# Row numbers, softmax factors and a scale read from a PSUM bank, and messages made four steps at once, in a graph and expert kernel

## The chip, the cores and the metric

The kernel runs on one core of one Trainium2 chip. The time is that of one execution on the device, in microseconds. Before the change it was 4558.61 us, the median of 3 runs (4550.4 to 4563.28).

## The reference

12,500 nodes with 256 features, 200,000 edges sorted by destination. Three blocks on the normalized rows, with residuals:

```python
xn = layernorm(x)
# 1 graph attention, 4 heads of 64
h = (xn @ W_src).reshape(n, 4, 64); a_src = (h * att_src).sum(-1); a_dst = ((xn @ W_dst).reshape(n, 4, 64) * att_dst).sum(-1)
e = leaky_relu(a_src[src] + a_dst[dst], 0.2)
p = exp(e - segment_max(e, dst)[dst])
out = segment_sum(p / segment_sum(p, dst)[dst] * h[src], dst) + bias     # then layernorm, prelu
# 2 linear attention with elu+1 features (8 heads of 32), merge, layernorm, a two-layer relu block on [xn, msg], layernorm(g2, b2)
# 3 eight experts of three layers with batch norm and relu, mixed by a softmax over the mean features
x = x + gat(xn) + mix(xn);  x = x + experts(layernorm(x))
```

## The kernel before, in words

There are three stages. A projection (up to about 340 us) computes the products of all nodes in chunks of 512 and writes the table `h_tab` (4 heads of 64 values and one source logit each, 260 words a node). Then comes the edge stage, and last the expert stage. The change is in the edge stage alone.

**Edge stage.** The edges are cut into 1664 steps of up to 128 edges, each of one destination tile of 128 nodes. 32 steps (`GS`) are a turn, and 4 steps (`GU`) a block `b`, so a turn has 8 blocks (`GQ`) and there are 52 turns. In turn g the engines aggregate the edges of turn g ("here") and prepare the softmax of turn g+1 ("ahead", q in the code); gathers and row numbers run up to two turns ahead. The second block, mix, advances in the same turns: one chunk of 512 nodes takes two turns, sixteen slots i = 0..15, so that even turns carry slots 0 to 7 and odd turns 8 to 15. These pairs of turns are what the rows below show. Slots 12 to 15 hold the four `hidden` products (L1487), 2 and 9 the output products (L1500), 7 and 8 `merge` (L1465).

**Order.** Nothing plans it: each engine has one function `turn` in which its work is written out by hand, block by block, and semaphores order the engines (`Stage.wait`, with counts per turn). Queues are first in, first out.

- POOL gathers the 128 rows of a step with one indirect DMA (L857) into `G[s]`, one of two buffers; it waits only for the aggregation of the same block two turns earlier (`g_mm`).
- DVE makes the one-hot matrices of a block (`onehot`, L391: the row of numbers 0 to 127 compared with each edge's relative destination), the chain of maxima, the logits (`dst_sums`, `exponents`, L935 to L949), the terms that shrink the running sum (`shrink`, L953 to L960; `shrunk`, L968), the weighted rows (`message`, L976: two steps at once, each gathered row times its softmax factor, which ACT has put in the row's 65th column) and the running sum (`add`, L991, each one on the one before it). It also serves mix: `o_scale` (L1043) times g2, `o_finish` (L1049) adds to the base, `quotients` (L1011), `deviations` (the norm's twelve small operations).
- ACT reads the source logits out of the gathered rows (`sources`, L1194, waits for all 32 gathers of the next turn), takes the exponent (L1208), turns a one-hot block to f32 (L1188) and empties PSUM for mix.
- PE transposes one-hots (L1338), looks up logits (L1349), aggregates (L1362: one-hot by weighted rows, step k into PSUM bank k mod 4, after the add that last read that bank) and computes mix's products. Banks 0 to 3 are used by the aggregation, 5 by mix.

Within a block DVE's order is: `message` of the next block's first half, add 0, `message` of its second half, add 1, the piece of work ahead, the mix slot, add 2, `onehot`, add 3, the rest of the mix slot. In the last block of a turn `dst_sums` and `exponents` stand first, then adds 0 and 1, `shrink` and both first messages of the next turn.

Of the kernel before, what the change touches and what calls it, by code (L numbers as in the profile page):

```python
# [5 lines left out]
P = 128  # L6
D = 256
HEADS = 4
KD = D // P
CH = 4  # L10
# [58 lines left out]
def build(nc, a, out, N, E):  # L69
# [13 lines left out]
    with es:  # L83
# [215 lines left out]
        T4 = ps[4][:, 0:D].bitcast(bf16)  # L299
        LB = 5  # L300
# [10 lines left out]
        o_norm, o_g, o_base = stage("o_norm"), stage("o_g"), stage("o_base")  # L311
# [15 lines left out]
        msg_set, g_mm, acc_add = stage("msg_set", 2 * GQ), stage("g_mm", GS), stage("acc_add", GS)  # L327
# [57 lines left out]
        def onehot(dve, q, sq, b):  # L385
# [6 lines left out]
                                    iota_row[:, :].unsqueeze(1).broadcast_to([P, GU, P]), d, ALU.is_equal  # L392
# [88 lines left out]
        def project_vector(dve):  # L481
# [133 lines left out]
            onehot(dve, 0, 0, 0)  # L615
            onehot(dve, 0, 0, 1)
# [190 lines left out]
        with nc.Block() as block:  # L807
# [55 lines left out]
            def _(dve):  # L863
# [13 lines left out]
                dve.wait_ge(ed_set, 1)  # L877

# [92 lines left out]
                def message(g, s, b, i):  # L971
# [69 lines left out]
                def o_scale(c):  # L1041
                    o_norm.wait(dve, c)
                    nc.vector.tensor_tensor(TM, TM, row(R_G2).unsqueeze(1).broadcast_to([P, CH, D]),  # L1043
                                            ALU.mult).then_inc(o_g.sem, 1)

                def o_finish(c):
                    o_g.wait(dve, c)
                    bx_in.wait(dve, c)
                    nc.vector.tensor_tensor(BX, BX, TM, ALU.add).then_inc(o_base.sem, 1)  # L1049

                def mix_between(n, i):
# [12 lines left out]
                    if prev and i == 14:  # L1064
                        o_scale(n - 1)
                    if prev and i == 15:
                        o_finish(n - 1)

                def mix_after(n, i):
# [4 lines left out]
                    if cur and i in (4, 5):  # L1074
                        quotients(n, i - 4)

                def turn(g, s, n, q, sq, nq, r):
# [5 lines left out]
                    for b in range(GQ):  # L1083
# [5 lines left out]
                        if here:  # L1089
                            if b < GQ - 1:  # L1090
                                message(g, s, b + 1, 0)
                            add(g, s, b, 0)
                            if b < GQ - 1:
                                message(g, s, b + 1, 1)
                            add(g, s, b, 1)
                        if ahead:
# [12 lines left out]
                            if b == GQ - 1:  # L1109
                                shrink(q, sq)  # L1110
                                message(q, sq, 0, 0)
# [995 lines left out]
```

## Time and profile before

| | us |
|---|---|
| median of the runs | 4558.61 |
| the profiled execution | 4551.85 |
| its span | 4549.9 |
| PE / DVE / ACT / POOL busy | 4134.0 / 3823.0 / 2277.0 / 1888.1 |
| mean granted clock of TensorE | 0.953 |

Busy times are sums over the span. A group of instructions has a line of the kernel, its count, its busy time and mean length, and the idle time of its engine just before it with what ended that. On a timeline, rows of the same kind that follow one another are merged; "x2" then means two, and the length runs from the first start to the last end.

### The profile page before, as it was taken

To read this page: it belongs to the slowest core of one execution; us is meant where nothing else is said; L and a number is where in the kernel's file an instruction comes from. 1 tells how busy PE (TensorE), PEld (TensorE's weight loads), DVE (VectorE), ACT (ScalarE), POOL (GpSimd) and SP (SyncE) were. 2 spreads that over 40 slices of the span, in tenths; PEclk is the share of its full clock that TensorE was granted. 3 is DMA by queue.
4 is the path that set the end of the run, shared out by engine and by line. 5 is a ranking of instruction groups with operands and counts; after the bars stand their busy time and mean duration, and the time that the engine had idled before them with its cause. 6 is when DMAs were issued, how large, how long until landed. Compare 5 with 4: busy or idle time off the path is not lost. (4 is left out here: it accounts for less than half of the span.)

```text
span 4549.9 us, 85744 instructions
## 1 busy us (share of the span) xinstructions
PE 4134.0 (91%) x23003; PEld 3316.4 (73%) x23004; DVE 3823.0 (84%) x9879; ACT 2277.0 (50%) x4346; POOL 1888.1 (41%) x1702
## 2 busy tenths in 40 slices
PE   8984898889988988998898884999999999999999
PEld 7873666666666666666666653888888888888888
DVE  8875889888988899898989886787887878878786
ACT  5552344344334334443434333666666666666666
POOL 2117777777777777777777730000000000000000
PEclk9996999999999999999999987999999999999999
DMA  5545777777777777777777753000000000000000
GB/s 193 170 142 149 206 205 227 213 209 208 226 211 208 210 223 208 208 221 218 210 206 220 211 164 93 23 21 28 14 28 20 22 28 14 28 24 19 28 14 19
DMA packets 440077, 601.76 MB, mean 132 GB/s; under 512 B 41560, under 2 KB 366704, under 8 KB 439920
## 3 DMA queue, kind: packets, MB, share of 16 engines
q1 hardware_dynamic: 360048, 378.47, 25.8%
q0 software_dynamic: 79872, 221.62, 19.7%
q8 instruction: 47, 0.77, 0.1%
q14 instruction: 110, 0.90, 0.1%
HBM read 312.68 MB, written 287.25 MB: 132 GB/s over the span
## 5 line engine op out<-in xcount | busy, mean ns | idle before, releaser
L857 POOL DMA_INDIRECT acc<-h_tab,strips x1664 | 1824.0, 1096 | 538.4 <-issue 518.0
L1362 PE MATMUL ps<-acc 128*128 128x260 f32 x3328 | 1011.1, 432 | 24.1 <-DVE acc L991 16.1
L991 DVE SCALAR_TENSOR_TENSOR acc<-acc,strips,ps 128x260 f32<-128x260 f32 x1664 | 792.4, 476 | 208.2 <-PE ps L1362 176.8
L1362 PEld LDWEIGHTS ps<-acc 128*128 128x128 f32 x3328 | 621.0, 207 | 112.7 <-DVE acc L991 22.4
L976 DVE TENSOR_TENSOR acc<-acc 128x512 f32<-128x512 f32 x832 | 562.6, 681 | 0.0
L1896 ACT ACTIVATE exp<-ps,bn 128x512 f32<-128x512 f32 (+1 forms) x400 | 310.2, 775 | 452.7 <-PE ps L1963 449.0
L1961 PE MATMUL ps<-w_hi,b_hi 128*128 128x256 f32 x1568 | 444.8, 284 | 1.2 <-DVE exp L1799 1.2
L1963 PE MATMUL ps<-w_hi,b_lo 128*128 128x256 f32 x1568 | 443.5, 283 | 0.0
L1962 PE MATMUL ps<-w_lo,b_hi 128*128 128x256 f32 x1568 | 443.5, 283 | 0.0
L1179 ACT ACTIVATE strips<-ps 128x512 bf16<-128x512 bf16 x416 | 247.6, 595 | 276.9 <-PE ps L1338 259.0
L1807 DVE TENSOR_TENSOR a_lo<-exp,a_hi 128x512 fp32r<-128x512 f32 (+1 forms) x400 | 258.7, 679 | 147.3 <-ACT a_hi L1898 132.2
L1487 PE MATMUL ps<-acc,keep 128*128 128x512 f32 x800 | 360.2, 593 | 0.0
L1813 DVE TENSOR_TENSOR b_lo<-exp,b_hi 128x512 fp32r<-128x512 f32 (+1 forms) x400 | 260.9, 677 | 113.4 <-ACT b_hi L1912 113.2
L1910 ACT ACTIVATE exp<-ps,bn 128x512 f32<-128x512 f32 (+1 forms) x400 | 311.3, 778 | 68.0 <-PE ps L1963 68.0
L1799 DVE SCALAR_TENSOR_TENSOR exp<-ps,exp 128x256 f32<-128x256 f32 x784 | 325.8, 476 | 20.0 <-issue 12.1
L1961 PE MATMUL ps<-x_hi,w_hi 128*128 128x512 f32 (+1 forms) x800 | 318.2, 398 | 17.9 <-ACT a_hi L1898 11.0
L1962 PE MATMUL ps<-x_lo,w_hi 128*128 128x512 f32 (+1 forms) x800 | 312.7, 391 | 0.0
L1963 PE MATMUL ps<-x_hi,w_lo 128*128 128x512 f32 (+1 forms) x800 | 311.1, 389 | 0.0
L1961 PE MATMUL ps<-a_hi,w_hi 128*128 128x512 f32 (+1 forms) x800 | 308.4, 386 | 0.6 <-ACT b_hi L1912 0.3
L1912 ACT ACTIVATE b_hi<-ps,bn 128x512 fp32r<-128x512 f32 (+1 forms) x400 | 308.6, 772 | 0.0
L1962 PE MATMUL ps<-a_lo,w_hi 128*128 128x512 f32 (+1 forms) x800 | 308.1, 385 | 0.0
L1963 PE MATMUL ps<-a_hi,w_lo 128*128 128x512 f32 (+1 forms) x800 | 307.8, 385 | 0.0
(271 smaller groups left out, 8325.5 us busy)
## 6 DMA issues: line engine op xcount, KB each, us to landing
side_tab<-acc SPq DMA_DIRECT2D x416, 520.0 KB
acc<-h_tab,strips POOLq DMA_INDIRECT x1664
acc<-xnt_tab SPq DMA_DIRECT2D x50, 512.0 KB
h_tab<-proj SPq DMA_DIRECT2D x25, 520.0 KB, 6.7
exp<-side_tab SPq DMA_DIRECT2D x100, 130.0 KB, 2.3
proj<-in_x SPq DMA_DIRECT2D x25, 512.0 KB, 5.3
base_tab<-proj SPq DMA_DIRECT2D x25, 512.0 KB, 3.2
xnt_tab<-proj SPq DMA_DIRECT2D x25, 512.0 KB, 6.0
```

Source lines behind the costliest of these rows:

```text
L857: pool.indirect_dma_start(G[s][:, b * GU + u], None, h_tab, bass.IndirectOffsetOnAxis(REC[s][:, b * GU + u, 0:1], 0)).then_inc(g_in[s], 16)
L976: nc.vector.tensor_tensor(m[:, :, :, 0:HB - 1], m[:, :, :, 0:HB - 1], m[:, :, :, HB - 1:HB].broadcast_to([P, 2, HEADS, HB - 1]), ALU.mult) ...
L991: nc.vector.scalar_tensor_tensor(A[:, (b % 2) * GU + u], A[:, (k - 1) % (2 * GU) if k else 2 * GU], smt[s][:, k:k + 1], ps[u][:, 0:MW], AL ...
L1362: nc.tensor.matmul(ps[u][:, 0:MW], S32[b % 2][:, u], G[s][:, b * GU + u], start=True, stop=True).then_inc(g_mm.sem, 1)
L1487: ins = nc.tensor.matmul(MIX[:, :], w1[:, k, m * P:(m + 1) * P], rhs, start=k == 0, stop=k == 3)
L1799: ins = nc.vector.scalar_tensor_tensor(Y[s][:, t], ps[4 + t // 2][:, (t % 2) * D:(t % 2 + 1) * D], WT8[s][:, t, e:e + 1], Y[s][:, t], ALU. ...
L1896: nc.scalar.activation(AR[:, m, cut(c)], ps[m][:, cut(c)], ACT.Relu, scale=bn[:, i:i + 1], bias=bn[:, 16 + i:17 + i])
L1910: nc.scalar.activation(BR[:, m, cut(c)], ps[2 + m][:, cut(c)], ACT.Relu, scale=bn[:, 32 + i:33 + i], bias=bn[:, 48 + i:49 + i])
L1912: nc.scalar.activation(BHI[e % 2][:, m, cut(c)], ps[2 + m][:, cut(c)], ACT.Relu, scale=bn[:, 32 + i:33 + i], bias=bn[:, 48 + i:49 + i]).th ...
L1961: nc.tensor.matmul(o, x[0], y[0], start=first, stop=False)
L1962: nc.tensor.matmul(o, x[0], y[1], start=False, stop=False)
L1963: return nc.tensor.matmul(o, x[1], y[0], start=False, stop=last)
```

## The change

A PSUM bank, number 3, is taken from the aggregation, which then rotates over banks 0 to 2. The bank holds the row of numbers (128 words), the softmax factors of the turn (128, `PF`, written by ACT in one more Exp) and g2 in two halves (2 x 128). `onehot` reads its numbers there (all but the first two calls of the program), `messages` its factors, `o_scale` its scale. `messages` makes four steps in one operation, and stands behind add 0. `o_scale` and `o_finish` each run in two halves, one before add 2 and one after add 3. A product of step k now waits for the add of step k-3, and at the head of a turn for the adds of steps 30 and 31.

```diff
+        BANKS = 3
+        IOTA_PS, PF = ps[BANKS][:, 0:P], ps[BANKS][:, P:2 * P]
+        G2_PS = [ps[BANKS][:, (2 + j) * P:(3 + j) * P] for j in range(2)]
@@ onehot
-                                    iota_row[:, :].unsqueeze(1).broadcast_to([P, GU, P]), d, ALU.is_equal
+                                    numbered.unsqueeze(1).broadcast_to([P, GU, P]), d, ALU.is_equal
@@ messages
-                    lo = b * GU + 2 * i
-                    m = G[s][:, lo:lo + 2].rearrange("p t (h c) -> p t h c", c=HB)
-                    nc.vector.tensor_tensor(m[:, :, :, 0:HB - 1], m[:, :, :, 0:HB - 1],
-                                            m[:, :, :, HB - 1:HB].broadcast_to([P, 2, HEADS, HB - 1]), ALU.mult
+                    lo = b * GU
+                    m = G[s][:, lo:lo + GU].rearrange("p t (h c) -> p t h c", c=HB)[:, :, :, 0:HB - 1]
+                    f = PF.rearrange("p (h t) -> p t h", h=HEADS)[:, lo:lo + GU]
+                    nc.vector.tensor_tensor(m, m, f.unsqueeze(3).broadcast_to([P, GU, HEADS, HB - 1]), ALU.mult
@@ add
-                                                   smt[s][:, k:k + 1], ps[u][:, 0:MW], ALU.mult, ALU.add
+                                                   smt[s][:, k:k + 1], ps[k % BANKS][:, 0:MW], ALU.mult, ALU.add
@@ o_scale, o_finish (h = 0 before add 2, h = 1 after add 3)
+                    v = TM[:, :, h * P:(h + 1) * P]
+                    nc.vector.tensor_tensor(v, v, G2_PS[h].unsqueeze(1).broadcast_to([P, CH, P]), ALU.mult).then_inc(o_g.sem, 1)
+                    t = slice(2 * h, 2 * h + 2)
+                    nc.vector.tensor_tensor(BX[:, t], BX[:, t], TM[:, t], ALU.add).then_inc(o_base.sem, 1)
@@ turn of DVE
-                            if b < GQ - 1:
-                                message(g, s, b + 1, 0)
                             add(g, s, b, 0)
                             if b < GQ - 1:
-                                message(g, s, b + 1, 1)
+                                messages(g, s, b + 1)
                             add(g, s, b, 1)
@@ ACT, once at the start
+                nc.scalar.activation(IOTA_PS, iota_row[:, :], ACT.Copy).then_inc(ps_set, 1)
+                for j in range(2):
+                    nc.scalar.activation(G2_PS[j], rows[:, R_G2 + j * P:R_G2 + (j + 1) * P], ACT.Copy).then_inc(ps_set, 1)
@@ ACT exponent
                     p_df.wait(act, q)
+                    msg_set.wait(act, q - 1)
+                    nc.scalar.activation(PF, df, ACT.Exp)
                     nc.scalar.activation(heads_of(sq), df.rearrange("p (h t) -> p h t", h=HEADS), ACT.Exp).then_inc(p_exp.sem, 1)
@@ PE aggregate
-                    msg_set.wait(pe, g, 2 * b + i + 1)
                     if i == 0:
+                        msg_set.wait(pe, g, b + 1)
                         s_ev.wait(pe, g, b + 1)
                     for u in (2 * i, 2 * i + 1):
-                        if b:
-                            acc_add.wait(pe, g, (b - 1) * GU + u + 1)
+                        k = b * GU + u
+                        if k >= BANKS:
+                            acc_add.wait(pe, g, k - BANKS + 1)
                         else:
-                            acc_add.wait(pe, g - 1, (GQ - 1) * GU + u + 1)
+                            acc_add.wait(pe, g - 1, 1 + max(j for j in range(GS) if j % BANKS == k))
```

## Rows read from the trace of the kernel before

**Rows 1.** The page: span and costliest groups (busy, mean ns, idle before).

```profile
span 4549.9 us, 85744 instructions
L857 POOL DMA_INDIRECT acc<-h_tab,strips x1664 | 1824.0, 1096 | 538.4 <-issue 518.0
L991 DVE SCALAR_TENSOR_TENSOR acc<-acc,strips,ps 128x260 f32<-128x260 f32 x1664 | 792.4, 476 | 208.2 <-PE ps L1362 176.8
L976 DVE TENSOR_TENSOR acc<-acc 128x512 f32<-128x512 f32 x832 | 562.6, 681 | 0.0
```

**Rows 2.** Windows (PE, PEld, DVE, ACT, POOL busy, clock, DMA): edge stage, its start.

```profile
340.00:2735.00 2395.00, 2090.05 (x10828) 1508.48 (x10828) 2095.68 (x5495) 928.45 (x2051) 1824.02 (x1664) 0.93 0.73 207
341.40:472.50 131.10, 66.79 (x361) 48.92 (x361) 80.45 (x229) 32.05 (x73) 101.60 (x97) 0.67 0.55 155
```

**Rows 3.** Timeline of POOL (start us, length us): a long gather and a short one.

```profile
1577.48 3.41 POOL L857 DMA_INDIRECT acc<-h_tab,strips  x1 [0.30 <-issue]
1581.19 0.95 POOL L857 DMA_INDIRECT acc<-h_tab,strips  x1 [0.30 <-issue]
```

**Rows 4.** Timeline of all engines, the end of an odd turn.

```profile
1573.71 2.00 PE L1362 MATMUL ps<-acc 128*128 128x260 f32 x8
...
1575.54 3.60 PE L1487 MATMUL ps<-acc,keep 128*128 128x512 f32 x8
...
1576.02 1.06 DVE L991 SCALAR_TENSOR_TENSOR acc<-acc,strips,ps 128x260 f32<-128x260 f32 x2
1576.13 0.44 ACT L1208 ACTIVATE acc<-strips 128x128 f32<-128x128 f32 x1 [1.12 <-DVE strips L949]
...
1577.32 0.33 DVE L957 TENSOR_SCALAR strips<-iota_row,strips 1x128 f32<-1x128 f32 x1
...
1577.65 1.27 DVE L976 TENSOR_TENSOR acc<-acc 128x512 f32<-128x512 f32 x2
1578.86 1.21 DVE L1049 TENSOR_TENSOR work<-work 128x1024 f32<-128x1024 f32 x1
...
1579.99 0.47 DVE L991 SCALAR_TENSOR_TENSOR acc<-acc,strips,ps 128x260 f32<-128x260 f32 x1
...
1580.39 0.67 DVE L391 TENSOR_TENSOR strips<-iota_row,strips 128x512 bf16<-128x512 f32 x1
...
1581.49 0.43 DVE L968 TENSOR_TENSOR acc<-acc,strips 128x260 f32<-128x260 f32 x1
...
1582.06 1.88 PE L1424 MATMUL ps<-acc,keep 128*128 128x512 f32 x4
```

**Rows 5.** Windows of four whole turns: odd, even, odd, even.

```profile
1442.40:1490.40 48.00, 43.31 (x209) 29.30 (x208) 42.10 (x118) 20.16 (x44) 37.64 (x35) 0.96 0.67 184
1490.40:1532.00 41.60, 37.76 (x215) 29.72 (x214) 38.40 (x96) 16.04 (x36) 32.46 (x31) 0.92 0.85 250
1532.00:1582.40 50.40, 45.69 (x210) 31.14 (x209) 42.34 (x117) 20.16 (x44) 39.48 (x36) 0.90 0.66 180
1582.40:1623.30 40.90, 36.36 (x215) 28.23 (x214) 38.31 (x96) 16.04 (x36) 32.02 (x30) 0.96 0.85 251
```

**Rows 6.** ACT's waits for gathers from 400 to 2700 us, and two on its timeline.

```profile
ACT strips L1194 <- DMA acc<-h_tab,strips: 37.7, 22, 10.6
...
472.55 0.43 ACT L1194 ACTIVATE strips<-acc 128x128 f32<-128x128 f32 x1 [3.69 <-DMA acc<-h_tab,strips]
...
1507.62 0.43 ACT L1194 ACTIVATE strips<-acc 128x128 f32<-128x128 f32 x1 [2.29 <-DMA acc<-h_tab,strips]
```

**Rows 7.** Groups of DVE from 400 to 2700 us: a PSUM input, 512 wide.

```profile
L1011 DVE TENSOR_TENSOR acc<-ps,work 128x512 f32<-128x512 f32 x50 | 34.2, 685 | 2.9 <-PE ps L1446 2.9
```

**Rows 8.** Timeline: DVE waiting for PE, and PE for ACT.

```profile
1527.70 1.99 PE L1465 MATMUL ps<-keep,acc 128*128 128x256 f32 x8 [0.56 <-ACT acc L1227]
...
1596.13 0.48 DVE L991 SCALAR_TENSOR_TENSOR acc<-acc,strips,ps 128x260 f32<-128x260 f32 x1 [1.40 <-PE ps L1362]
```

**Rows 9.** Timeline of PE behind `deviations`, and the window around it.

```profile
1548.58 0.61 PE L1338 MATMUL ps<-strips 128*128 128x128 bf16 x4 [3.60 <-DVE strips L391]
...
1547.30:1557.40 10.10, 8.25 (x33) 6.75 (x34) 9.35 (x24) 6.23 (x12) 7.96 (x8) 0.50 0.72 196
```

More of the change, by code:

```diff
@@ L310, in build @@
         ln_ag, ln_rs, ln_nb = stage("ln_ag"), stage("ln_rs", RSQ), stage("ln_nb")
-        o_norm, o_g, o_base = stage("o_norm"), stage("o_g"), stage("o_base")
+        o_norm, o_g, o_base = stage("o_norm"), stage("o_g", 2), stage("o_base", 2)
         win_in, win_f, pick_set, rec_mm, rec_ev = (stage("win_in", 16), stage("win_f"), stage("pick_set"), stage("rec_mm"),
@@ L326, in build @@
         rs_set, rs_mm, rs_exp, rs_done = stage("rs_set", 5), stage("rs_mm"), stage("rs_exp"), stage("rs_done")
-        msg_set, g_mm, acc_add = stage("msg_set", 2 * GQ), stage("g_mm", GS), stage("acc_add", GS)
+        msg_set, g_mm, acc_add = stage("msg_set", GQ), stage("g_mm", GS), stage("acc_add", GS)
         bn_st = stage("bn_st", 2 * (RSQ + 2))
@@ L383, in select, with onehot @@
                                            ALU.is_equal).then_inc(pick_set.sem, 1)
-        def onehot(dve, q, sq, b):
+        def onehot(dve, q, sq, b, numbered):
             dr_set.wait(dve, q)
@@ L614, in project_vector @@
             relative(dve, 0, 0)
-            onehot(dve, 0, 0, 0)
-            onehot(dve, 0, 0, 1)
+            onehot(dve, 0, 0, 0, iota_row[:, :])
+            onehot(dve, 0, 0, 1, iota_row[:, :])
             for k in range(KC):
@@ L877, in _ @@
                 dve.wait_ge(ed_set, 1)
+                dve.wait_ge(ps_set, 3)
                 def gaps(q):
@@ L1039, in deviations, with o_scale, o_finish @@
                                                    ).then_inc(ln_nb.sem, 1)
-                def o_scale(c):
+                def o_scale(c, h):
                     o_norm.wait(dve, c)
-                    nc.vector.tensor_tensor(TM, TM, row(R_G2).unsqueeze(1).broadcast_to([P, CH, D]),
-                                            ALU.mult).then_inc(o_g.sem, 1)
-                def o_finish(c):
+                    v = TM[:, :, h * P:(h + 1) * P]
+                    nc.vector.tensor_tensor(v, v, G2_PS[h].unsqueeze(1).broadcast_to([P, CH, P]), ALU.mult).then_inc(o_g.sem, 1)
+                def o_finish(c, h):
                     o_g.wait(dve, c)
                     bx_in.wait(dve, c)
-                    nc.vector.tensor_tensor(BX, BX, TM, ALU.add).then_inc(o_base.sem, 1)
+                    t = slice(2 * h, 2 * h + 2)
+                    nc.vector.tensor_tensor(BX[:, t], BX[:, t], TM[:, t], ALU.add).then_inc(o_base.sem, 1)
                 def mix_between(n, i):
@@ L1064, in mix_between @@
                     if prev and i == 14:
-                        o_scale(n - 1)
+                        o_scale(n - 1, 0)
                     if prev and i == 15:
-                        o_finish(n - 1)
+                        o_finish(n - 1, 0)
                 def mix_after(n, i):
@@ L1075, in mix_after @@
                         quotients(n, i - 4)
+                    if prev and i == 14:
+                        o_scale(n - 1, 1)
+                    if prev and i == 15:
+                        o_finish(n - 1, 1)
                 def turn(g, s, n, q, sq, nq, r):
@@ L1110, in turn @@
                                 shrink(q, sq)
-                                message(q, sq, 0, 0)
-                                message(q, sq, 0, 1)
+                                messages(q, sq, 0)
                         if here:
@@ L1116, in turn @@
                         if ahead and b < GQ - 2:
-                            onehot(dve, q, sq, b + 2)
+                            onehot(dve, q, sq, b + 2, IOTA_PS)
                         if q2 is not None:
@@ L1120, in turn @@
                                 relative(dve, q2, 1 - sq)
-                                onehot(dve, q2, 1 - sq, 0)
+                                onehot(dve, q2, 1 - sq, 0, IOTA_PS)
                             if b == GQ - 1:
-                                onehot(dve, q2, 1 - sq, 1)
+                                onehot(dve, q2, 1 - sq, 1, IOTA_PS)
                         if here:
```

5 lines of the change are left out of this document (3 added, 2 removed).

## The prediction, made before the change was run

> **What bounds the kernel now.** I read first the times and the page's busy table, then the windows by stage, the costliest groups, the waits of ACT, and last the timelines around one group of steps. The span is 4549.9 us [rows 1] inside an execution of 4551.85 us; the median shown is 4558.61, so 6.8 us are added at the end to come from this execution to the median. The edge stage lasts 2395 us, from 340 to 2735 [rows 2]. The change touches no instruction of the projection before it or of the expert stage behind it, so only these 2395 us can move.
>
> In the edge stage PE is busy 87% and DVE 88%, so neither is simply the bound. The third engine is POOL. It issues 1664 gathers of 1096 ns mean, with 518 us of "issue" in front [rows 1]; that is 1.41 us each, 2342 us in all, nearly the whole stage. A gather that meets nothing takes 0.95 us and 0.30 us of issue, 1.25 us [rows 3]. So 0.15 us x 1664 = 250 us are excess, and the reader sees where it comes from in one long gather, 3.41 us from 1577.48 [rows 3]: beside it DVE runs L957, L960, two L976 and L1049, all with SBUF inputs only, and the gather ends 0.90 us after L991 starts at 1579.99, the first DVE operation in a while that has an input in PSUM [rows 4]. POOL is held by DVE's operations with two inputs in SBUF, and let go by one that reads PSUM.
>
> The Trainium skill speaks of this in "SBUF — State Buffer", section "Who interferes with whom": a VectorE instruction with two SBUF inputs contends with a GpSimd instruction that reads SBUF, one with a single SBUF input does not; but it infers that descriptor generation is not touched by `tensor_tensor`. The first half agrees with the 3.41 us gather, the inference does not: by it the excess would not be there and the gathers would stay at 1.10 us after the change.
>
> Does that excess set the stage's time? Mostly not. Turns (32 steps each, from one `shrunk` to the next) come in pairs, 40.9 and 48.0 us when nothing disturbs, 41.6 and 50.4 when something does [rows 5]. Two turns of POOL are 64 x (1.10 + 0.30) = 89.6 us, against 88.9 for an undisturbed pair. So POOL and the DVE/PE loop run at almost the same pace, and DVE and PE have their own 88.9. ACT waits for gathers (L1194) 37.7 us in 22 waits [rows 6]; the first is 10.6 us, the second 3.69, and only those near 2.3 us, as at 1507.62 [rows 6], go with a turn of 41.6 (five turns).
>
> **The change, part by part.**
>
> (1) Gathers. `onehot` (8 a turn), `message` and `o_scale` read one input from PSUM and no longer hold POOL. What still does are the scans, L957/L960, L968, L997, L1049 and the short ones. I take 80% of the excess as gone: 1.25 + 0.03 = 1.28 us, 41 us a turn, below the 44.4 of the loop; POOL stops being a bound. Worth at the start: 97 gathers took 101.6 us busy until 472.5 [rows 2], 9.4 us over 97 x 0.95; the second turn's sources end that chain, with a wait of 3.69 us at 472.55 [rows 6]. 70% of 9.4 is 6.5 us. In the middle: five turns of 41.6 come down to 40.9, 0.7 x 5 = 3.5 us. Bounds: 0 (if PSUM doesn't free POOL) and 9.4 + 3.5.
>
> (2) DVE's wide operations. A 512-wide `tensor_tensor` costs the same from SBUF (L976: 562.6 us over 832, 676 to 681 ns [rows 1]) as with a PSUM input (685, L1011 [rows 7]), so I charge nothing for the bank. Bounds: below, nothing can be gained by a bank whose rows are no shorter, 0; above, an add of 260 with a PSUM input is 476 ns (L991 [rows 1]) and the 260-wide L968 from SBUF 430 ns [rows 4], 46 ns x 882 operations = 41 us. No row shows the strided factors that `messages` reads (PF, 32 words apart between heads). I take 0, by L1011, the nearest in shape. The Trainium skill, "VectorE: DVE Perf Modes", section "The TRN2 errata", gives a VectorE operation 120 cycles of fixed cost from PSUM and 58 from SBUF; by that each would pay an estimated 65 ns more, 882 x 65 ns = 57 us of DVE time. The trace's L1011 doesn't show it.
>
> (3) Two messages of 512 become one of 1024. Start to start a 512 takes 0.60-0.61 us (two L976 at 1577.65, next start 1578.86 [rows 4]) and a 1024 takes 1.13 us (L1049 at 1578.86, next 1579.99). Saved 0.08 us per four steps, 1.3 us a pair. But messages now stand behind add(b,0), so add(b,3) and add(b+1,0) meet. Two adjacent adds start 0.58 us apart (1.06 less 0.48), an add with another operation behind it 0.40 (1579.99 to 1580.39) [rows 4]: 0.18 us lost at 9 of the 14 inner boundaries of a pair (the others have `quotients`, `denominators`, `dst_sums` or `o_scale`/`o_finish` between), and 0.2 at each `shrunk`, which add(0,0) now follows at once. Where DVE waits for PE anyway (about half of them) this is free: 0.18 x 4 + 0.2 x 2 = 1.1 a pair. `o_scale` and `o_finish` in halves: 2 x 0.07 = 0.14. DVE nets zero: -1.3 + 1.1 + 0.14. Bounds -1.3 and +1.9 a pair.
>
> (4) Three banks. A product k now needs add(k-3), before add(k-4), and the first two of a turn need the add before the last and the last. Queued behind it on PE: the transposes, the mix products, `shrink`. For most steps PE has over 0.2 us in hand. Not for the last product of a turn (k=31), which needs add(7,0), run only after `exponents`: PE did all four at 1573.71 and went to `hidden` at 1575.54, add(7,0) ends at 1576.50 [rows 4]. `hidden` then starts at about 1576.85, 1.3 us late. DVE reaches `shrunk` by then at the old time, for half of L1049 is still to be done there, so most is hidden; what is left is that add(0,0) ends about 0.1 us before and product 3 of the next turn waits for it: q_product from 1582.06 [rows 4] to about 1582.7, 0.6 us. That reaches DVE at step 3, where it waits for PE (1.40 us at 1596.13 [rows 8]). In an even turn `merge` waits for ACT anyway (0.56 us at 1527.70 [rows 8]). Between, DVE's shorter messages give 0.5 back. Bounds: 0 and 2.5 us a pair (1.3 + 0.6 + 0.6, nothing absorbed).
>
> (5) ACT. A second Exp of 128x128 stands before the one of 0.44 us (L1208, 1576.13 [rows 4]) and moves its end from 1576.57 to about 1576.9. `messages(q,0)` starts at 1577.65, so it is hidden there; but `attended` behind it in the even turn moves by 0.3, and PE waits for it. 0.3 us a pair; bounds 0 and 0.44.
>
> (4) and (5) make 0.6 - 0.5 + 0.3 = 0.4, say 0.45 us a pair with rounding of DVE's side, x 25 = 11 us.
>
> (6) The clock. A turn of 48.0 us has a granted clock of 0.96 and one of 50.4 has 0.90 [rows 5]. In the second PE stands idle for 3.60 us behind `deviations` until 1548.58 [rows 9], and the clock is at its lower level, 1.2 GHz (0.50), from 1547.3 to 1557.4; in most turns that stretch is 3.4 us. Seven of 25 pairs have the long one (turns of 50.4 to 50.8), five of them behind a late gather. If half of these five go, 2.5 x 2.4 = 6 us less. Bounds: 7 x 2.4 = 17 less (all go), 18 x 2.4 = 43 more (all pairs get it).
>
> Sum: -6.5 - 3.5 + 0 + 11 - 6 = -5 us on the profiled execution, 4547; plus 6.8 gives 4553.6. I forecast 4553 us, no change that can be told (a change within 0.3%, 14 us, is about what a measurement of this kernel can't tell from none).
>
> **Rivals.**
> A, the forecast: gathers shorten, the loop of DVE and PE doesn't. 4553; own range 4538 to 4570. For it: 88.9 us pairs run without any late gather. Against it: the terms are small against what the clock can do.
> B, faster: with POOL's holds gone every odd turn is 48.0 and every even one 40.9. 7 x 2.4 + 3.5 + 9.4 = 30 us less, with (4) and (5) hidden, and 3 more of DVE's shorter messages: 4525. For it: five of the long stretches follow a late gather. Against it: two don't.
> C, slower: the third bank's loss. PE's head start is eaten where DVE still has `exponents` to run, and nothing absorbs it: (1.3 + 0.6) x 25 = 48 us, less the 10 of POOL: 4558.6 + 38 = 4597. It decides from the point where product 31 waits over 1 us and `shrunk` waits for it. For it: PE works without a gap from 1573.71 to 1579.14 [rows 4], so a late start there has nothing to hide in. Against it: the half of L1049 that moves behind add(7,3) gives PE 0.6 us.
> D, slower: the PSUM operand isn't free: the 41 us of (2), half to all of it on the path, 4574 to 4594. For it: the strided read has no row, and L991 against L968. Against it: L1011.
> E, the gathers don't shorten at all, since what holds POOL is not the second SBUF input: then there is no term of (1) or (6), +11 in all: 4570. For it: one long gather is one case, and the L1011 kind of operation is rare, so the trace shows few gathers beside one. Against it: that gather ends with L991's start.
>
> **Chances.** A 0.41, B 0.32, C 0.15, D 0.07, E 0.05. Faster by over 0.3%: B and 0.01 of A's tail, 0.33. Slower: C, D and 0.04 of the tails of A and E, 0.26. Within: the rest, 0.41. The range takes in B, with the same again below it (all long stretches gone and DVE's saving), and C: 4510 to 4600.
>
> **What would show it.** Gathers (L857's line) near 0.98 us mean instead of 1.10, and for the first time waits of POOL for PE's products; L1194 waiting for gathers only in the first turns; the message row at about 1.2 us x416; 680 to 690 ns for `onehot`. For (4): PE waits for L991's line at product 31 of each turn, and PE's `hidden` starting over a microsecond after the fourth product. Turn pairs between 88.5 and 90. The prediction is wrong if pairs fall under 88 (then DVE's or POOL's share was larger than I read), or if DVE's wait for PE's aggregate products (176.8 us of idle now, [rows 1]) rises by over 40 us.

## The result: 3.0% slower

The changed kernel takes 4697.77 us (median of 4, 4687.6 to 4698.52) beside 4559.73 for the kernel before: ratio 1.0301, interval 1.028 to 1.0322. I had forecast 4553, range 4510 to 4600, so the time lies 98 us above the range. Its page (columns as in [rows 1]) has these lines:

```profile
span 4695.7 us, 84910 instructions
...
PEclk9996899999999999999999997999999999999999
...
L861 POOL DMA_INDIRECT acc<-h_tab,strips x1664 | 1600.7, 962 | 878.0 <-issue 510.9
L1376 PE MATMUL ps<-acc 128*128 128x260 f32 x3328 | 1049.2, 436 | 212.7 <-DVE acc L996 204.0
L996 DVE SCALAR_TENSOR_TENSOR acc<-acc,strips,ps 128x260 f32<-128x260 f32 x1664 | 792.6, 476 | 350.4 <-PE ps L1376 329.8
...
L982 DVE TENSOR_TENSOR acc<-acc,ps 128x1024 f32<-128x1024 f32 x416 | 504.4, 1213 | 0.1
```

Against [rows 1]: gathers fell from 1096 to 962 ns and the message row from 562.6 to 504.4 us busy, both as meant. But DVE's idle before `add` rose from 208 to 350 us. The waits from 400 to 2800 us (who waits for whom: us in total, times, longest) name the two sides of one loop, and a third engine that now has time to spare:

```profile
POOL acc L861 <- PE ps L1376: 367.1, 216, 6.5
DVE acc L996 <- PE ps L1376: 322.4, 246, 3.0
PEld ps L1376 <- DVE acc L996: 277.2, 252, 5.2
...
PE ps L1376 <- DVE acc L996: 190.6, 136, 4.5
```

In the kernel before PE waited for `add` 10.3 us in 28 waits over 400 to 2700. DVE and PE now wait for each other, POOL for PE.

Where the 145.8 us between the two profiled spans lie is read from the start of the last `add`: 2733.1 us before, 2864.4 after. The edge stage has 131.3 of them, and the expert stage behind it, whose code is unchanged, 14.5. (The medians of all executions lie 138.0 apart: the profiled execution of the kernel before was 8 us under its median.) A turn and its partner, before [rows 5] and here (windows, columns as in [rows 2]):

```profile
1455.79:1498.91 43.12, 37.19 (x216) 27.15 (x215) 38.07 (x87) 16.24 (x38) 29.96 (x33) 1.00 0.83 243
1498.91:1551.37 52.46, 46.02 (x213) 31.12 (x210) 41.92 (x111) 20.36 (x45) 31.55 (x33) 0.90 0.59 166
```

A pair is 95.6 us, against 88.9 to 92.0. DVE's busy time in it did not grow (80.4 before, 80.0 here): on DVE all of the loss is waiting.

### What stands in a turn

The end of an odd turn on PE, the place of [rows 4] (timeline: start, us, engine, line, operation, idle before):

```profile
1542.79 1.26 PE L1376 MATMUL ps<-acc 128*128 128x260 f32 x5
1545.72 0.71 PE L1376 MATMUL ps<-acc 128*128 128x260 f32 x2 [1.67 <-DVE acc L996]
1546.26 3.60 PE L1501 MATMUL ps<-acc,keep 128*128 128x512 f32 x8
...
1552.45 1.88 PE L1438 MATMUL ps<-acc,keep 128*128 128x512 f32 x4
1554.46 0.32 PE L1383 MATMUL ps<-ident,strips 128*128 128x128 f32 x1
1554.65 0.58 PE L1362 MATMUL ps<-strips 128*128 x4
...
1555.59 1.14 PE L1376 MATMUL ps<-acc 128*128 128x260 f32 x4
```

The last product of the turn waits 1.67 us for `add(7,0)`, which stands behind `exponents`; `hidden` (L1501) starts behind it, `q_product` (L1438) behind that, and only then the products of block 1. DVE pays at the end of the row (DVE's timeline):

```profile
1554.48 0.48 DVE L996 SCALAR_TENSOR_TENSOR acc<-acc,strips,ps 128x260 f32<-128x260 f32 x1
1556.33 0.48 DVE L996 SCALAR_TENSOR_TENSOR acc<-acc,strips,ps 128x260 f32<-128x260 f32 x1 [1.37 <-PE ps L1376]
```

Before, `add(1,0)` did not wait here. Where else the time went is read from the starts of `add(b,0)` over turns 6 to 47. From one start to the next is an interval; a pair of turns has 16 (b = 0 to 7 of the even turn, then of the odd one), and each is given as its median. The first grew from 3.58 to 4.96 us, the second of the odd turn from 5.74 to 6.68, and its fourth and fifth from 4.66 and 5.59 to 6.31 and 7.04. The last two are where PE's clock falls:

```profile
1516.44 1.24 PE L1376 MATMUL ps<-acc 128*128 128x260 f32 x2 [3.94 <-DVE acc L996]
1517.47 0.63 PE L1351 MATMUL ps<-strips 128*128 128x128 bf16 x4
1517.89 2.05 PE L1376 MATMUL ps<-acc 128*128 128x260 f32 x4
...
1521.66 1.12 PE L1490 MATMUL ps<-ident,work 128*128 128x128 f32 x4 [0.56 <-ACT acc L1258]
```

```profile
1516.00:1526.50 10.50, 9.50 (x36) 7.59 (x37) 8.72 (x21) 6.21 (x12) 4.46 (x5) 0.52 0.57 172
```

PE stands idle 3.94 us behind `deviations` (3.60 in [rows 9]) and is then granted 1.2 GHz (0.52 in that window) for 10.2 us. Between 500 and 2550 us there are 19 stretches of 10.2 us in the changed kernel, 7 before. That is not more time at the lower clock. The mean granted clock of the edge stage is 0.93 in both ([rows 2], and here):

```profile
340.00:2880.00 2540.00, 2148.60 (x10829) 1500.30 (x10828) 2090.78 (x5165) 939.57 (x2106) 1600.68 (x1664) 0.93 0.68 197
```

Summed over the stage, 293 us are at 1.2 GHz in the kernel before and 286 in the changed one. Before, most of it is in stretches of 3.4 us (43 between 500 and 2550 us, 4 here); here nearly all of it follows this one wait.

### The profile page after: what moved, and what is told of

Read it like the earlier page. It is cut to its first block and busy times, and to the rows that moved or that the text cites. A ratio compares the mean times of both kernels' runs of the same rounds, so it can differ in the third digit from the quotient of the medians.

```text
span 4695.7 us, 84910 instructions
## 1 busy us (share of the span) xinstructions
PE 4199.7 (89%) x23003; PEld 3312.3 (71%) x23004; DVE 3810.8 (81%) x9513; ACT 2288.1 (49%) x4401; POOL 1663.7 (35%) x1702
## 5 line engine op out<-in xcount | busy, mean ns | idle before, releaser
L861 POOL DMA_INDIRECT acc<-h_tab,strips x1664 | 1600.7, 962 | 878.0 <-issue 510.9
L1376 PE MATMUL ps<-acc 128*128 128x260 f32 x3328 | 1049.2, 436 | 212.7 <-DVE acc L996 204.0
L996 DVE SCALAR_TENSOR_TENSOR acc<-acc,strips,ps 128x260 f32<-128x260 f32 x1664 | 792.6, 476 | 350.4 <-PE ps L1376 329.8
L1376 PEld LDWEIGHTS ps<-acc 128*128 128x128 f32 x3328 | 602.1, 206 | 363.7 <-DVE acc L996 291.1
L982 DVE TENSOR_TENSOR acc<-acc,ps 128x1024 f32<-128x1024 f32 x416 | 504.4, 1213 | 0.1
L1501 PE MATMUL ps<-acc,keep 128*128 128x512 f32 x800 | 359.6, 592 | 0.0
```

What stands on the lines that cost most here:

```text
L861: pool.indirect_dma_start(G[s][:, b * GU + u], None, h_tab, bass.IndirectOffsetOnAxis(REC[s][:, b * GU + u, 0:1], 0)).then_inc(g_in[s], 16)
L982: nc.vector.tensor_tensor(m, m, f.unsqueeze(3).broadcast_to([P, GU, HEADS, HB - 1]), ALU.mult).then_inc(msg_set.sem, 1)
L1376: nc.tensor.matmul(ps[k % BANKS][:, 0:MW], S32[b % 2][:, u], G[s][:, b * GU + u], start=True, stop=True).then_inc(g_mm.sem, 1)
L1501: ins = nc.tensor.matmul(MIX[:, :], w1[:, k, m * P:(m + 1) * P], rhs, start=k == 0, stop=k == 3)
```

## The experiments

Intervals below are medians worked out from the starts of `add(b,0)`, turns 6 to 47, as above. The diffs are cut to the lines that matter. "Edge" is the start of the last `add`, "tail" the span from there to the end; before has 2733.1 and 1816.8.

### e1: three banks alone

```diff
-    nc.tensor.matmul(ps[u][:, 0:MW], ...           # after acc_add of step k-4
+    nc.tensor.matmul(ps[k % BANKS][:, 0:MW], ...   # BANKS = 3, after acc_add of step k-3
```

> The kernel before with one edit: the aggregation rotates over banks 0 to 2, so that product k waits for add(k-3) and the first two products of a turn for the adds of steps 30 and 31. Bank 3 is unused, nothing else changes. Theory 1 (the third bank's loss makes the time, and the clock's long stretch follows from it): 4650 to 4720 us, DVE's idle time for PE's aggregation products rises from 177 to over 300 us, and the stretch at half speed is the long one in most pairs of turns. Theory 2 (the loss comes from the wide messages and their place behind add 0, or from the PSUM operands): under 4590 us.

4608.66 us beside 4557.14, ratio 1.0113 (1.0096 to 1.013): 51 us, between the two expectations. A pair (windows):

```profile
1427.11:1470.37 43.26, 40.01 (x216) 29.45 (x216) 38.56 (x96) 16.09 (x37) 32.51 (x32) 0.92 0.81 243
1470.37:1519.71 49.34, 44.13 (x208) 28.77 (x208) 42.18 (x117) 20.14 (x44) 34.98 (x34) 0.97 0.64 176
```

The medians of the turns are 42.5 and 49.4, 91.9 a pair against 88.9. Two intervals carry it: the first of the even turn 4.90 us (+1.32) and the second of the odd one 6.78 (+1.04), 2.36 of the 3.0. Edge is 2796.0 (+62.9 beside a profiled execution of before that was 6.8 us under the median of 4558.61), and DVE's idle time for PE's aggregation products is 247.6 us (176.8 before), under the 300 of theory 1. The long stretch at half speed is not part of it: between 500 and 2550 us there is none of 10.2 us here. So the third bank's loss is real and is 2.4 us a pair in these two intervals alone, with nothing of it absorbed.

### e2: the operands from SBUF again

```diff
-    f = PF.rearrange(...)[:, lo:lo + GU]
+    f = G[s][...][:, :, :, HB - 1:HB]       # onehot and o_scale too; no second Exp
```

> The changed kernel with its operands taken from SBUF again: onehot from iota_row, messages from the 65th column of the gathered rows, o_scale from rows, and without the second Exp. Three banks, wide messages and the halves stay. Theory 1: gathers are back at 1.08 to 1.12 us mean, but POOL is hidden behind a loop that is slower than it, so 4680 to 4720 us, within 0.5% of the changed kernel. Theory 2 (PSUM operands or the second Exp cost): 30 us or more below the changed kernel.

4695.08 us, 1.0305 (1.0288 to 1.0322), the changed kernel's time, though its gathers are long:

```profile
L861 POOL DMA_INDIRECT acc<-h_tab,strips x1664 | 1852.6, 1113 | 626.4 <-issue 505.8
```

962 to 1113 ns, and nothing follows: theory 1. What the bank operands cost on DVE and ACT and what they give on POOL is zero together in this kernel; POOL waits for PE in it anyway (367.1 us above). The second Exp goes together with the operands here, so that neither has a price of its own.

### e3: the wide message alone

```diff
-    message(g, s, b + 1, 0); add(g, s, b, 0); message(g, s, b + 1, 1); add(g, s, b, 1)
+    add(g, s, b, 0); messages(g, s, b + 1); add(g, s, b, 1)      # SBUF factors, four banks
```

> The kernel before with messages of four steps behind add 0, from SBUF, and all four banks. Theory 1: within 0.5% of the kernel before (4540 to 4580 us). Theory 2 (the order of DVE's work costs): over 4600 us. A theory of the clock alone says that any shift may lock the long stretch in, about 4590 us.

4624.61 us, 1.015 (1.0133 to 1.0166): 67 us. This edit I had priced at nothing. The pair is 92.7 us. The fourth and fifth intervals of the odd turn are 5.86 and 6.60 (+2.2), the sixth and seventh of the even one 6.33 and 6.46 (+1.3), with DVE idle 0.76 us (median) before `add(6,0)` where it did not wait. Edge grew by 58.7 and tail by 11.9. PE's granted clock in the edge stage is 0.92, where e1 has 0.95 and the kernel before 0.93:

```profile
340.00:2800.00 2460.00, 2106.60 (x10828) 1515.95 (x10828) 2084.14 (x5097) 927.05 (x2051) 1876.00 (x1664) 0.92 0.69 202
```

Gathers are 1127 ns (1876.0 us over 1664): a wide message from SBUF holds POOL longer, not shorter, than two halves. This is a rival for the 67 us. The ends of every 64th gather lie 92.0 us apart in e3 and 90.1 before, and POOL runs further and further ahead of the adds (from 31 to 43 us), so 92.0 is its own pace. A loop that had lost nothing could not have gone below that: some 50 of the 59 us in the edge stage would have come by POOL alone. That e3's pairs take 92.7 shows a loss in the loop, but e3 can't say what the order costs by itself. In the changed kernel POOL is not in the way, and i1 measures it there.

### e4: the changed kernel with the clock's gap filled

```diff
+    if cur and i == 10:        # PE, odd turn, behind deviations
+        for _ in range(4): nc.tensor.matmul(MIX[:, :], ident[:, :], w1[:, 0, :], start=True, stop=True)
```

The four products of 512 columns are read by nobody.

> The changed kernel, and in slot 10 of mix, where PE otherwise stands idle behind deviations, four more products of 512 columns into mix's bank whose results nobody reads. If the stretch at half speed comes from that idle time, the granted clock of odd turns rises from about 0.90 to 0.96 or more and the time falls by 2 to 4 us a pair, 50 to 100 us, to 4600 to 4650. If the clock is not what the odd turns are longer by, no change or slower by the 3.6 us of the products: 4700 to 4780.

4611.17 us, 1.0118 (1.0101 to 1.0135): 87 us less than the changed kernel, for work added.

```profile
1429.87:1472.99 43.12, 38.54 (x216) 28.33 (x215) 38.07 (x87) 16.25 (x38) 29.80 (x33) 0.96 0.80 243
1472.99:1522.48 49.49, 45.80 (x220) 29.21 (x218) 41.91 (x110) 20.36 (x45) 31.64 (x33) 1.00 0.62 177
```

The odd turn has a clock of 1.00 and 49.5 us instead of 52.4; the fourth and fifth intervals are 4.86 and 5.56 again, and PE's longest idle there is 1.18 us. Edge is 63.9 us less than in the changed kernel, tail 20.4 less (more on the tail under i1).

### f1: the same filler in the kernel before

> The kernel before with the same four unread products of PE in slot 10 of mix, behind deviations. The changed kernel lost 87 us by them. If the clock's long stretch is what sets the odd turns of 50.4 us apart from those of 48.0, all odd turns come to about 48.0 or less and the time falls by 7 x 2.4 = 17 us or more, to 4500 to 4540. If PE has no slack in those turns, 4555 to 4600.

4554.43 beside 4560.16, 0.999 (0.998 to 0.9999), far from the first expectation and just under the range of the second. Odd turns shorten to 47.5 us, even ones lengthen to 42.8: 90.2 a pair. The gathers stay at 1098 ns with the same issue, 1.41 us each, and 64 x 1.41 = 90.2. ACT waits for gathers 82.2 us in 30 waits (37.7 in 22 before, [rows 6]). The kernel before stands on POOL's pace as well as on its loop; its long stretches cost next to nothing, because what they cost is slack against POOL.

### f2 and f4: the wide message ahead of add 0

```diff
-    add(g, s, b, 0)
     if b < GQ - 1: messages(g, s, b + 1)
+    add(g, s, b, 0)
```

> The kernel before with messages of four steps, but ahead of add 0, where the first half stood. Theory 3 (what cost 67 us in the kernel with wide messages alone is their place: the message ahead of add(b,0) covered DVE's wait for PE's first product of the block): back to 4530 to 4565 us, and DVE's idle time for PE's aggregation products falls from 230 to 180 us or less. Rival (one operation of 1024 is itself what costs, since add 1 comes later in any place): 4600 us or more.

f2 (four banks, SBUF factors): 4602.91, 1.0094 (1.0078 to 1.0111), 22 us less than e3: the time that the rival expected, but with the idle time of theory 3, 175.1 us.

> The changed kernel with messages ahead of add 0. Theory 3 alone: 50 to 70 us below the changed kernel, 4630 to 4650. Against it stands theory 1: add(b,0) is 1.1 us later, and product 3 of each block waits for it in a kernel with three banks, so that the gain is eaten: 4680 to 4720.

f4 (the changed kernel): 4661.4 (4648 to 4694), 1.0229 (1.0178 to 1.028), 36 less than the changed kernel, with odd turns of 52.8 in most pairs; its four executions lie 45 us apart, so the 36 are rough. The place of the message is a part of its cost in both. What is left in f2 can't be put down to the width in the loop: its gathers are 1123 ns, POOL's pace (read as in e3) and the mean of the pairs of turns are both 91.7 us, and ACT waits for gathers 92.7 us in 33 waits. So f2 stands on POOL, which is how its DVE can wait no longer for PE than before and its time still be 43 us longer. What the width costs in the loop alone no run separates.

### f3: the irregular bank change moved inside the turn

```diff
+    bank = lambda k: (k + (k >= 24)) % BANKS     # the head of a turn then needs k-3, not k-2
```

> The changed kernel with the rotation's irregular place moved: instead of the first two products of a turn it is steps 24 and 25 that wait for the add two steps back, and the first three of a turn wait for add(k-3). If the wait of product 1 for the last add of the turn before is what makes the head of a turn late (DVE idle 1.4 us before add(1,0), and again in slot 9), 20 to 50 us below the changed kernel, 4650 to 4680. If the head is late because of product 31 and product 3, which wait for adds behind exponents and shrunk, no change within 10 us.

4693.66, 1.0293 (1.0276 to 1.031): no change. The first products of a turn, which need the add before the last and the last one, are not what is late. Products 31 and 3 are left, which wait in both; that it is they is read from these waits and tested by no run of its own on such a chip.

### g1 to h4: eight runs on two chips with other waits

g1 and h1 turn one order round: `add(7,0)` ahead of `dst_sums` and `exponents`. g2 and h2 put the two halves of the message back in their old places, with factors from PSUM, in the changed kernel. g3 does both; g4 and h4 add e4's filler to g3, h3 adds it to h2.

```diff
-    messages(g, s, b + 1)
+    message(g, s, b + 1, 0); add(g, s, b, 0); message(g, s, b + 1, 1)   # g2; factors PF[:, lo:lo+2]
-    dst_sums(q); exponents(q); add(g, s, 7, 0)
+    add(g, s, 7, 0); dst_sums(q); exponents(q)                          # g1
```

> The changed kernel with one order turned on VectorE: in block 7 of a turn add(7,0) runs ahead of dst_sums and exponents, not behind them. Theory 1 (the last product of a turn, which needs add(7,0)'s bank, waits behind exponents, and PE's queue behind it is late): PE's 1.67 us wait at that product shrinks to under 0.8, hidden starts about 0.5 us earlier in each of 50 turns, 10 to 35 us less: 4660 to 4688. Theory 2 (the two products at the head of a turn and the message behind add 0 carry the whole loss): the wait goes but the time stays within 6 us of 4694.

> The changed kernel with its message of 1024 columns taken apart again: two of 512 in the places of the kernel before (ahead of add 0 and between add 0 and add 1), their factors still from the PSUM bank; three banks stay. Theory 1 (the two losses add up: 51 us for three banks, 67 for the message behind add 0): 4605 to 4635, close to the kernel before with three banks alone (4609), and the long half-speed stretch leaves most pairs. Theory 2 (the bank operands, which free POOL, are worth something once the message no longer stands in the way): 4570 to 4600, below three banks alone. Theory 3 (with three banks the order of the messages is worth little, since the message behind add 0 only costs where the fourth bank has been counted on): above 4660.

> Both edits together: two messages of 512 in the old places with factors from PSUM, and add(7,0) ahead of dst_sums and exponents; three banks. Theory 1: what the third bank costs is mostly the last product of each turn, so 15 to 35 us below the run with the halves alone: 4580 to 4600. Theory 2 (the head's product 3 and the look's queue carry it): within 8 us of the run with the halves alone.

> The same, and four 512-column products whose result nobody reads, put on PE at step 10 of an odd turn, where PE stands idle behind deviations, so that the clock does not fall there for 10 us. Theory 1 (POOL is no longer what holds a pair at 89.6 us, since its gathers are near 1.0 us; only PE's order and its clock do): pairs fall under 89 us, 4520 to 4550, below the kernel before. Theory 2 (three banks cost what the relief of POOL gives): 4555 to 4590. Theory 3 (the long stretch is already absent once the halves are back): within 8 us of the run without the filler.

> The changed kernel with add(7,0) ahead of dst_sums and exponents instead of behind them, on another chip than g1. Theory 1 (the last product of each turn, and what PE has queued behind it, is a large part of the loss): hidden starts about 0.5 us earlier in each of 50 turns, 4660 to 4688. Theory 2 (the products at the head of a turn and the message behind add 0 carry it): within 8 us of the changed kernel's 4694 to 4698.

> The changed kernel with two messages of 512 in the places of the kernel before, factors still from the PSUM bank, three banks. Theory 1 (the two losses add up): 4605 to 4635, as the kernel before with three banks alone (4609). Theory 2 (POOL's relief is worth something once the message no longer stands in the way): 4570 to 4600. Theory 3 (with three banks the messages' order is worth little): above 4660.

> h2 with four 512-column products whose result nobody reads, on PE at step 10 of an odd turn, where it stands idle behind deviations. Theory 1 (the clock's long stretch is what h2 still has over the kernel before): 4550 to 4580. Theory 2 (the halves have already taken the long stretch away in most pairs, as in the kernel before with three banks alone): within 10 us of h2.

> h3 and add(7,0) ahead of dst_sums and exponents. Theory 1 (with POOL relieved, the clock filled and the last product early, nothing of the three banks' loss is left but the head's): 4525 to 4555, below the kernel before. Theory 2 (three banks cost what POOL's relief gives): 4555 to 4600.

| | us | before on that chip | ratio |
|---|---|---|---|
| g1 | 5082.3 | 4975.8 | 1.0212 (1.0169 to 1.0256) |
| g2 | 5120.7 | 4975.8 | 1.0285 (1.0244 to 1.0326) |
| g3 | 5108.8 | 4975.8 | 1.0260 (1.0218 to 1.0303) |
| g4 | 5132.7 | 4975.8 | 1.0326 (1.0284 to 1.0368) |
| h1 | 5136.7 | 5024.6 | 1.0225 (1.0193 to 1.0257) |
| h2 | 5164.2 | 5024.6 | 1.0281 (1.0235 to 1.0327) |
| h3 | 5163.8 | 5024.6 | 1.0275 (1.0241 to 1.0309) |
| h4 | 5156.9 | 5024.6 | 1.0264 (1.0232 to 1.0297) |

None of the absolute times expected came, and none of the theories is settled by these runs: the kernel before itself takes 9 to 10% longer on these two chips. h1's waits over 400 to 3100 us show why the runs can't be set beside the others:

```profile
ACT strips L1192 <- remote: 296.7, 111, 6.2
DVE acc L996 <- remote: 239.3, 104, 6.7
```

"remote" is a semaphore raised from outside the engines, most likely by a transfer's end; the changed kernel's own waits over the same time have no such row. With turns of 55 us each another loop bounds the stage, and its ratios say nothing of this one: the same halves that cost 2.8% here cost 0.7% on the next chip. What holds these semaphores back there stays open.

### i1: the halves back, three banks, factors from PSUM

The kernel of g2 and h2, on a chip where before takes 4557.55.

> The kernel of g2 and h2 on another chip: the changed kernel with two messages of 512 in the places of the kernel before, factors from the PSUM bank, three banks. Where both kernels wait for late transfers it was 1.028 of before, no better than the changed kernel on a good chip. Theory 1 (the two losses add up): 4605 to 4635. Theory 2 (POOL's relief shows): 4570 to 4600. Theory 3 (with three banks the place of the message is worth little): above 4660.

4592.22, 1.0072 (1.0055 to 1.0088): in the range of theory 2. That is 105 us below the changed kernel for one edit, and 16 below e1, which differs by the bank operands, the second Exp and the halves of `o_scale` and `o_finish`. Theory 2's reason holds for 12 of the 16 us, those of the edge stage; the rest is the tail, which has nothing to do with POOL (below).

```profile
1424.67:1466.99 42.32, 37.36 (x216) 27.19 (x215) 38.27 (x97) 16.15 (x38) 29.73 (x32) 1.00 0.84 245
1466.99:1516.43 49.44, 44.07 (x209) 28.86 (x208) 42.22 (x120) 20.43 (x46) 32.20 (x33) 0.97 0.63 179
```

```profile
L861 POOL DMA_INDIRECT acc<-h_tab,strips x1664 | 1612.8, 969 | 790.3 <-issue 502.7
```

Turns 6 to 47 last 1935.0 us, e1's 1935.4: POOL's relief gives nothing there, for the 91.9 us of the three banks' loop are over POOL's own 64 x 1.37 = 88 in e1. The 12 us of edge come before and behind these turns. PE at the place of the long stretch:

```profile
1483.98 0.70 PE L1379 MATMUL ps<-acc 128*128 128x260 f32 x2 [3.43 <-DVE acc L996]
```

3.43 us of idle instead of 3.94, and no stretch of 10.2 us between 500 and 2550 us. From i1 to the changed kernel, edge grows by 80.2 us. e4 takes 63.9 of them away by filling the idle stretch; 16 are left for the cover that the message no longer gives. The tail grows by 22.6. There the waits of the last 1800 us differ in rows of PE's own issue, in the changed kernel:

```profile
PEld ps L1975 <- issue: 24.1, 13, 4.5
...
PE ps L1975 <- issue: 16.9, 10, 1.8
```

and in i1:

```profile
PEld ps L1978 <- issue: 5.0, 2, 4.5
```

Ten times, 143 us apart, PE waits 1.4 to 1.8 us for nothing that the profile shows. The stage is written as a loop of eleven passes over two chunks each (`ring`), so it goes back to its start ten times. The pages of the two kernels differ in one more row there, queue 8 of the DMA list, of the kind "instruction" (packets, MB, share). The changed kernel, then i1:

```profile
q8 instruction: 136, 2.23, 0.2%
```

```profile
q8 instruction: 47, 0.77, 0.1%
```

Behind the last `add` this queue moves 106 packets of 16 KB in the changed kernel and 16 in i1; in the middle of the stage it moves 86 and none. So in each pass of the loop instructions are brought in again that i1 brings in once. All eight kernels with the wide message and no filler (the changed one, e2, e3, f2, f3, f4, g1, h1) have 136 packets, the ten waits of PE and a tail of 1827 to 1833 us; the other twelve have 47 and none of these waits. Among them the kernel before, e1 and f1 have ten waits of DVE instead:

```profile
DVE exp L1799 <- issue: 12.1, 10, 1.4
```

Their tails are 1816 to 1818 us, those of the other nine 1809 to 1813. The code of the stage is the same in all; what differs is the code ahead of it. That the waits go with instruction transfers is shown by this; that the place of the loop in the program decides it is an inference, for no run moved the code alone.

### i2: all edits together

The kernel of g4 and h4: i1, `add(7,0)` ahead of `exponents`, and the filler.

> The kernel of g4 and h4 on another chip: i1, add(7,0) ahead of dst_sums and exponents, and the four unread products at step 10. Theory 1 (with POOL relieved, the clock filled and the last product early, only the head's loss is left): 4525 to 4555. Theory 2 (three banks cost what POOL's relief gives): 4555 to 4600.

4624.71, 1.0146 (1.0129 to 1.0163): both theories wrong, it is 32 us slower than i1. The odd turn takes 49.2 us, i1's 49.4, so the filler gives nothing where no long stretch is; the even turn goes from 42.8 to 44.3. There the seventh and eighth intervals are 5.14 and 8.25 us, 13.4 together, against 11.3: with `add(7,0)` in front of it, `exponents` waits for PE's product first (DVE idle 1.0 us before `add(7,0)`), and `shrink` and the next turn's first messages stand behind it. The late last product is cheaper than a late `exponents`. The two edits of i2 were not run one by one on such a chip. No version with a part of the change beats the kernel before; f1, which has none of it, is 6 us below it.

## Why the prediction was wrong

**What bounds the kernel.** Read right in kind, too loosely in size. POOL and the loop of DVE and PE do run at one pace, and f1 shows how close: 90.2 us a pair. The prediction had both numbers for POOL, 1.41 us a gather and 1.10 + 0.30; only the second, 89.6 a pair, went into the comparison. The kernel before takes 89.9 a pair on average over turns 6 to 47, which is POOL's pace and not the loop's 88.9. That also meant that only a shorter loop could bring a gain, and the change made it longer.

**(1) Gathers.** Right: 962 ns against "near 0.98", POOL waits for PE, and e2 ties it to the second SBUF input of the wide operations. Its worth is at most the edge stage of i1 against e1, 12 us, where I had 10. The inference weighed there, of the Trainium skill, "SBUF — State Buffer", section "Who interferes with whom", that `tensor_tensor` leaves descriptor generation alone, doesn't agree with 962 against 1113 ns in two kernels that differ by those operands and the second Exp. Rival E is out.

**(2) PSUM operands at nothing.** Right: `onehot` 681 ns, `messages` 1213 ns for 1024 with factors from PSUM, and e2, which also drops the second Exp of (5), lies 3 us from the changed kernel. Rival D is out. (5) by itself was not measured: no run drops the second Exp alone.

**(4) Three banks: mis-sized.** The mechanism came as told: `hidden` is 1.56 us late against the start of `add(7,0)` (1.3 forecast), and `q_product` behind it. I then let DVE's spare work absorb most of it, 0.45 a pair with (5); e1 measures 3.0 a pair, 2.4 of it in two intervals, against an upper bound of 2.5. The error is in "`q_product` later by 0.6". It is 1.2 (1.5 in e1), the products behind it are late with it, and that reaches `add(1,0)` of the even turn, which did not wait before, and not step 3, where DVE waits anyway. 25 x 2.4 = 60 us: rival C's mechanism, at 0.15. Its number, 4597, is close to what three banks with the operands measure, 4592, in part by luck: 8 us of i1's time are gained in the expert stage, which C does not speak of.

**(3) Wide messages at zero: the step that failed.** I counted DVE's busy time (-1.3 + 1.1 + 0.14 a pair) and that part is right: DVE's busy time fell by 0.4 a pair. I did not ask what PE has to do meanwhile. A message of 512 ahead of `add(b,0)` gave PE the first two weighted rows of the next block a whole add and half a message earlier, and it was work that DVE did while PE finished `add(b,0)`'s product. Behind the add and in one piece it does neither. In place of zero, i1 against the changed kernel measures 105 us for this step. Little of it is the lost cover itself. Most comes by a path that I had not joined to this step: PE's idle behind `deviations` grows from 3.43 to 3.94 us, the long stretch at 1.2 GHz follows in nearly every pair, and e4 takes 64 us away by filling that idle. 23 are the expert stage. My own sign of being wrong came too: DVE's wait for PE's aggregation products was to rise by no more than 40 us, and rose from 176.8 to 329.8.

**(6) The clock.** "All pairs get it" was my upper bound, 43 us, and I put -6 in the sum. Nearly all pairs got it, and e4 measures 64 us in the edge stage. The bound itself was short: 2.4 us was the difference of two odd turns in a kernel which waits for POOL in either, as f1 shows; without POOL's pace in the way the stretch costs 2.9 us a pair. Nor does it go with a late gather, as I had argued: no gather is late here. What differs ahead of it is PE's idle behind `deviations`. Over the 21 odd turns from 7 to 47 it is 3.92 to 3.94 us here, with a stretch of 10.2 us in 19; 3.54 to 3.81 in the kernel before, with 7; 3.37 to 3.44 in i1, with none. The length alone does not decide: in the kernel before an idle of 3.55 us stands before stretches of 3.4 and of 10.2 us, and e3, with 4.14 to 4.22, has the long one in 11 of 21. What else decides stays open.

**Not in the sum.** 14.5 us in the expert stage, which I had excluded since its code is untouched: ten waits of PE that come, less ten of DVE that go.

Closing the account, from profiled spans: before to i1 +51.1 edge (banks, less POOL's relief, and some 8 us by which these two profiled executions, 43 us apart, differ more than the medians, 35) and -8.1 tail (DVE's ten waits gone), i1 to the changed kernel +63.9 clock, +16.3 lost cover, +22.6 tail: 145.8, the whole difference. The split between clock and cover assumes that e4's filler removes the stretch and nothing else. It removes more than i1 lacks (time at 1.2 GHz in the edge stage: 286 us in the changed kernel, 194 in i1, 133 in e4), but the intervals that it shortens are the two behind the stretch, and i1's odd turn, 49.4 us, is close to e4's 49.5.

## What to carry to other kernels

Two engines that hand work to each other in order are a loop: price a moved or merged operation by when its consumer's first piece is ready and by what wait of its own engine it was covering, not by its duration. A buffer taken from such a loop can cost its longest detour between two uses in full, where the queue behind it has no slack (2.4 us a pair here); go through the queue to the next operation of the other engine that does not wait today. Where some turns already show a lower clock and an edit lengthens the idle time in front of it, put the full penalty in the sum, not the mean. And when a run of one part alone makes another engine slower, as e3's wide messages did to POOL, its time is no price of that part.

## What the runs showed of the hardware

- Four products more that nobody reads made the changed kernel 87 us faster, by filling a 3.94 us idle stretch of PE; the granted clock of the odd turn rose from 0.90 to 1.00. In the kernel before the same four gave 6 us.
- The mean granted clock of the edge stage was 0.93 before and after. What cost time was where the lower clock fell, not how much of it there was.
- A gather beside wide DVE operations takes 962 ns where these read one input from PSUM, 1065 to 1127 where both are in SBUF.
- A stage with unchanged code took 1809 to 1813, 1816 to 1818 or 1827 to 1833 us in kernels that differ only ahead of it: without waits for issue in its loop, with ten of DVE (1.1 to 1.4 us), with ten of PE (1.3 to 1.9 us). Those of PE go with 136 packets on the instruction queue 8 instead of 47.
- Of the five chips of the experiments, two ran the kernel before at 4976 and 5025 us instead of 4557 to 4560, with waits for "remote" semaphores.
